# A gated cross-attention kernel on one core: FFN maximum taken chunk by chunk, second half of the queries moved into the attention loop, GpSimd's key splits moved later

## What is computed

```python
x = x + tanh(g_xattn[0]) * dtw_align(ctx, layernorm(x))      # dynamic time warping, traced back
x = x + tanh(g_ffn[0])   * bit_ffn(layernorm(x))             # below
x = x + tanh(g_xattn[1]) * attention(layernorm(x), ctx)      # 16 heads of 16, softmax over 375 keys
x = x + tanh(g_ffn[1])   * pattern_ffn(layernorm(x))         # 2048 patterns, three top-k selections
```

## Time and profile before

| what | value |
|---|---|
| median of 3 runs | 580.42 us (579.89 to 580.88) |
| the profiled execution's own time | 581.3 us |
| its span | 579.6 us |
| mean granted TensorE clock | 0.835 of full |
| busy TensorE / VectorE / ScalarE / GpSimd | 403.9 / 414.0 / 261.1 / 81.3 us |

### The profile page before, as it was taken

The page is one execution under the profiler, slowest core; times in us unless marked ns, Lnnn a source line. Parts: engine busy times, 40 slices in busy tenths (PEclk is TensorE's granted clock), DMA queues, the critical chain, the costliest instruction groups (busy, mean ns, idle before and its releaser), DMA issues.

```text
span 579.6 us, 10039 instructions
## 1 busy us (share of the span) xinstructions
PE 403.9 (70%) x3352; PEld 268.5 (46%) x3356; DVE 414.0 (71%) x1680; ACT 261.1 (45%) x674; POOL 81.3 (14%) x209
## 2 busy tenths in 40 slices
PE   2898799722249799787899999999999602503106
PEld 2557586511137455454577776676545300202003
DVE  7644999999965758997988887784354575375773
ACT  3854444712231543246465555765453352353440
POOL 6791000000024063724000000000000000000000
PEclk9998799955559799799999999999999955855556
DMA  9700003287004688410034847920860000000002
GB/s 271 230 1 1 0 2 120 94 174 158 14 2 132 105 153 159 128 50 1 2 54 69 217 68 139 185 79 2 332 247 1 1 0 2 0 1 1 1 1 63
DMA packets 33448, 47.22 MB, mean 81 GB/s; under 512 B 5477, under 2 KB 29942, under 8 KB 32246
## 3 DMA queue, kind: packets, MB, share of 16 engines
q1 hardware_dynamic: 33398, 46.58, 32.9%
HBM read 37.87 MB, written 8.60 MB: 80 GB/s over the span
## 4 chain that ended last, share of the span: by engine, by line
PE 45%; DVE 33%; ACT 12%; issue 5%; POOL 4%; DVEq 0%; POOLq 0%; ACTq 0%
PE ps L2118 8%; ACT below L1726 6%; PE ps L2082 5%; DVE PR L1028 4%; PE ps L2069 4%; PE ps L2058 4%; PE ps L1967 4%; PE ps L2044 3%; DVE R L962 2%; PE ps L1912 2%; DVE prod L1024 2%; PE ps L1828 2%; DVE PR L1026 2%; PE ps L2239 1%; DVE R L958 1%
## 5 line engine op out<-in xcount | busy, mean ns | idle before, releaser
L1242 DVE TENSOR_REDUCE negm<-ps 112x1 f32<-112x375 f32 x128 | 65.5, 543 | 9.2 <-PE ps L2058 6.0
L1700 ACT ACTIVATE E<-ps 125x448 f32<-125x448 f32 x96 | 52.0, 544 | 40.9 <-PE ps L2069 40.6
L2207 PE MATMUL ps<-cnt,same 128*128 128x7 bf16 (+3 forms) x36 | 6.2, 171 | 70.9 <-ACT below L1726 62.8
L2058 PE MATMUL ps<-ks,qs 96*112 96x375 bf16 x128 | 42.8, 345 | 1.7 <-DVE negm L1242 0.8
L1230 DVE TENSOR_REDUCE acts<-gel 128x4 f32<-128x448 f32 x32 | 19.8, 621 | 31.2 <-ACT gel L1668 31.2
L2082 PE MATMUL ps<-E,v 125*32 125x112 f32 x768 | 42.0, 270 | 0.0
L2069 PE MATMUL ps<-qs,ks 99*125 99x112 bf16 x384 | 39.4, 225 | 1.2 <-DVE qs L1263 0.7
L2069 PEld LDWEIGHTS ps<-qs,ks 99*125 99x125 bf16 x384 | 33.7, 137 | 10.2 <-issue 6.2
L2207 PEld LDWEIGHTS ps<-cnt,same 128*128 128x128 bf16 (+1 forms) x36 | 4.0, 111 | 73.6 <-issue 73.6
L1668 ACT ACTIVATE gel<-ps 128x448 f32<-128x448 f32 x32 | 17.3, 544 | 29.3 <-PE ps L2118 29.3
L768 POOL CAST kp<-kx 128x750 bf16<-128x750 f32 x8 | 6.5, 812 | 163.5 <-ACT path L1583 125.1
(11 more groups left out here) (369 smaller groups left out, 1037.7 us busy)
## 6 DMA issues: line engine op xcount, KB each, us to landing
ks<-key_parts SPq DMA_DIRECT2D x48, 187.5 KB, 6.7
piwT<-fn_process_input_weights SPq DMA_DIRECT2D x4, 2048.0 KB, 14.9
key_parts<-kp SPq DMA_DIRECT2D x48, 93.8 KB
ctx_again<-in_ctx SPq DMA_DIRECT2D x7, 512.0 KB
keys<-kx SPq DMA_DIRECT2D x16, 187.5 KB, 2.2
kx<-keys SPq DMA_DIRECT2D x8, 375.0 KB, 6.0
ctxP<-in_ctx SPq DMA_DIRECT2D x8, 256.0 KB, 6.4
patT<-in_L_ffn_input_patterns SPq DMA_DIRECT2D x1, 2048.0 KB, 13.2
```

Source lines behind the costliest of these rows:

```text
L1242: drain(dve.tensor_reduce(negm[:, n:n + 1], bank(nm)[0:S, 0:SC], AX.X, ALU.max, negate=True), nm)
L1700: drain(fn(E[:, (KCH * f + c) % 6, :], bank(nm)[0:KC, 0:4 * S], ACT.Exp), nm)
L2058: fill(mm(bank(nm)[0:S, 0:SC], qs[0:SR, u // 4 % 3, n, :], ks[0:SR, u // 4 % 3, n, :], start=True, stop=True), nm)
```

## The change

Three edits, put in together.

1. **FFN maximum.** ScalarE writes the absolute value of chunks 0 to 5 back into their slots of `ct0`. VectorE takes a running maximum of those, five maxima of two tensors, each one chunk behind the middle tap. `hmax2` is gone. TensorE's transposes of the maximum stand ahead of the fillers, of which four are left of ten.
2. **Queries.** Before the loop only the first half is transposed, multiplied, biased and split. The second half's transposes stand in round -4, its products and ScalarE's copies in rounds -3 and -2; three fillers a round are left only in round -1. Its split goes from VectorE to GpSimd, behind the keys of batch 4.
3. **Keys of batches 5 to 7.** GpSimd splits them after the far queries and the bias adds. SyncE stores the parts of batch b + 2 and loads the keys of batch b + 4 behind the stack of batch b.

```diff
+EARLY = 5
...
-            for b in range(2, B):
+            for b in range(2, EARLY):
                 store_parts(b)
-                if b + 2 < B:
-                    load_keys(b + 2)
+                load_keys(b + 2)
                 if b == 2:
                     load_stack(2)
             for b in range(3, B):
                 wait_filled(sp, ("scoreT", 4 * b - 9, KCH - 1))
                 load_stack(b)
+                if b + 2 < B:
+                    store_parts(b + 2)
+                    if b + 4 < B:
+                        load_keys(b + 4)
...
             wait_drained(pool, ("ffn_up", 0, 1))
-            for b in range(2, B):
+            for b in range(2, EARLY):
                 split_keys(b)
+            for t in range(2):
+                wait_drained(pool, ("qT", t, 1))
+                far = slice(448, 896)
+                did(pool.tensor_tensor(qx32[:, t, far], qx32[:, t, far], qp[:, t, 0, far], ALU.subtract))
+                settle()
+                did(pool.tensor_copy(qp[:, t, 1, far], qx32[:, t, far]))
+                settle()
+                pool.tensor_tensor(qp[:, t, 2, far], qx32[:, t, far], qp[:, t, 1, far], ALU.subtract
+                                   ).then_inc(q_far_split, 1)
             wait_drained(pool, "bo")
             pool.wait_ge(ln_ready, 3 * B)
             for b in range(B):
                 pool.tensor_tensor(x[:, b, :], x[:, b, :], gbo[:, :], ALU.add).then_inc(bias_added, 1)
+            for b in range(EARLY, B):
+                split_keys(b)
...
                     if e >= 3:
                         dve.wait_ge(silu_done, e - 2)
+                        settle()
...
-                if c in (5, 8):
-
-                    e = c - 5
-                    dve.wait_ge(silu_done, e + 3)
-                    three = hs[:, e:e + 3, :].rearrange("p c t -> p t c")
-                    if e == 0:
-                        ins = dve.tensor_reduce(hmax[:, :], three, AX.X, ALU.max, apply_absolute_value=True)
+                if 4 <= c < HT + 1:
+
+                    e = c - 3
+                    dve.wait_ge(size_ready, e + 1)
+                    if e == 1:
+                        ins = tt(hmax[:, :], ct0[:, 0, :], ct0[:, 1, :], ALU.max)
                     else:
-                        did(dve.tensor_reduce(hmax2[:, :], three, AX.X, ALU.max, apply_absolute_value=True))
                         settle()
-                        dve.wait_ge(hmax_part, 1)
-                        ins = tt(hmax[:, :], hmax[:, :], hmax2[:, :], ALU.max)
-                    ins.then_inc(hmax_part, 1)
+                        ins = tt(hmax[:, :], ct0[:, e % 3, :], hmax[:, :], ALU.max)
+                    if e < HT - 3:
+                        did(ins)
+                    else:
+                        ins.then_inc(hmax_ready, 1)
...
-            for half in range(2):
-                for t in range(2):
-                    wait_drained(dve, ("qT", t, half))
-                    cols = slice(448 * half, 448 * half + 448)
...
+            near = slice(0, 448)
+            for t in range(2):
+                wait_drained(dve, ("qT", t, 0))
...
                 fn(hs[:, c, :], ct0[:, c % 3, :], ACT.Silu, bias=cb[:, c:c + 1]).then_inc(silu_done, 1)
                 if c + 3 < HT:
                     spread_taps(c + 3)
+                if c < HT - 2:
+                    act.wait_ge(silu_done, c + 1)
+                    fn(ct0[:, c % 3, :], hs[:, c, :], ACT.Abs).then_inc(size_ready, 1)
...
-            query_columns(0)
-            norm_columns(1)
-            query_columns(1)
+            query_columns(0, 0)
+            query_columns(0, 1)
...
                 if f == -3:
                     load_table(ACT.Exp)
+                if f == -4:
+                    norm_columns(1)
+                if f in (-3, -2):
+                    query_columns(1, f + 3)
...
-            keep_clock(("hidT", HT - 1, 0), 10)
-            pe.wait_ge(hmax_part, 2)
+            pe.wait_ge(hmax_ready, 1)
             hidden_transposes(("hmaxT",), hmax)
+            keep_clock(("hidT", HT - 1, 0), 4)
...
+            ln_transposes(2, "lnT2", ln2, 0)
+            query_product(0, 0)
+            query_product(0, 1)
...
-                pe.wait_ge(q_split, 2 * (u // (2 * B)) + tile + 1)
+                pe.wait_ge(q_split if u < 2 * B else q_far_split, tile + 1)
...
-                if f < 0:
+                if f == -4:
+                    ln_transposes(2, "lnT2", ln2, 1)
+                if f in (-3, -2):
+                    query_product(1, f + 3)
+                if f == -1:
                     keep_clock(("pv", 0), 3)
```

More of the change, by code:

```diff
@@ L360, in build_program @@
         hmax = rf.take("hmax", [128, TOK])
-        hmax2 = rf.take("hmax2", [128, TOK])
         q2 = Region(q2_at).take("q2", [128, HT, TOK], BF16)
@@ L485, in build_program @@
          qx_ready, sx_ready, scaled, norm_ready, rows_ready, q2_act, uu_ready, rounded, bias_added, cand_ready,
-         signs_ready, dg_ready, silu_done, s2_ready, q2_ready, hmax_part,
-         neg_ready, q_split, k_split, pv_part, cnt_ready, tie_ready, sel_ready,
+         signs_ready, dg_ready, silu_done, size_ready, s2_ready, q2_ready, hmax_ready,
+         neg_ready, q_split, q_far_split, k_split, pv_part, cnt_ready, tie_ready, sel_ready,
          gel_ready, gel_used, acts_ready, pmx_ready, pmd_ready, pexp_ready, vec, scl, pol) = [sem(n) for n in (
@@ L491, in build_program @@
              "sx_ready scaled norm_ready rows_ready q2_act uu_ready rounded bias_added cand_ready signs_ready "
-             "dg_ready silu_done s2_ready q2_ready hmax_part neg_ready q_split "
+             "dg_ready silu_done size_ready s2_ready q2_ready hmax_ready neg_ready q_split q_far_split "
              "k_split pv_part cnt_ready tie_ready sel_ready gel_ready gel_used acts_ready "
@@ L1211, in _ @@
                 normalise(b, x, ln2[:, b, :])
-            for half in range(2):
-                for t in range(2):
-                    wait_drained(dve, ("qT", t, half))
-                    cols = slice(448 * half, 448 * half + 448)
[L1217 to L1221, removed]
+            near = slice(0, 448)
+            for t in range(2):
+                wait_drained(dve, ("qT", t, 0))
+                did(tt(qx32[:, t, near], qx32[:, t, near], qp[:, t, 0, near], ALU.subtract))
+                settle()
+                did(dve.tensor_copy(qp[:, t, 1, near], qx32[:, t, near]))
+                settle()
+                tt(qp[:, t, 2, near], qx32[:, t, near], qp[:, t, 1, near], ALU.subtract).then_inc(q_split, 1)
             a0 = quarters(acts[0][:, :])
@@ L1642, in norm_columns, with query_columns @@
                     drain(fn(ln2T[:, h, 448 * half:448 * half + 448], bank(nm)[:, 0:448], ACT.Copy), nm)
[L1644 to L1652, removed]
+            def query_columns(half, t):
+                nm = ("qT", t, half)
+                wait_filled(act, nm)
+                cols = slice(448 * half, 448 * half + 448)
+                did(fn(qx32[:, t, cols], bank(nm)[:, 0:448], ACT.Identity, bias=bqs[:, t:t + 1], scale=HD ** -0.5))
+                drain(fn(qp[:, t, 0, cols], bank(nm)[:, 0:448], ACT.Identity, bias=bqs[:, t:t + 1],
+                         scale=HD ** -0.5), nm)
             half_root(2, 0)
@@ L2023, in _, with query_product @@
                 keep_clock(("lnT2", 0, 0), 3)
-            for half in range(2):
-                ln_transposes(2, "lnT2", ln2, half)
+            def query_product(half, t):
+                nm = ("qT", t, half)
+                claim(pe, nm)
                 for h in range(DH):
                     wait_drained(pe, ("lnT2", h, half))
[L2028 to L2034, removed]
+                    ins = mm(bank(nm)[:, 0:448], wqT[:, h, 128 * t:128 * t + 128],
+                             ln2T[:, h, 448 * half:448 * half + 448], start=(h == 0), stop=(h == DH - 1))
+                fill(ins, nm)
+            ln_transposes(2, "lnT2", ln2, 0)
+            query_product(0, 0)
+            query_product(0, 1)
             def queries(u):
```

## The result

The changed kernel took 579.34 us (median of 20 runs, 573.44 to 583.24) against 581.35 for the kernel before (20 runs, 579.89 to 583.65): a ratio of 0.9949, 95% interval 0.9928 to 0.9970. The ratio leaves out the changed kernel's three longest runs, counted as a slower state since they lie over 1.5% above its fastest; the medians of all twenty differ by 2.0 us. So it is faster by a third to a half of a per cent, a third to a half of the 6 us that were forecast, and its runs spread more widely than those before. The profiled execution took 580.88 around a span of 579.2. What the runs at 573 to 576 lost, no profile shows.

A forecast was written before the change was run, and what follows sets the result against it. TensorE was taken to bound convolution and early attention, VectorE leading between until the quantised hidden is out. Terms -6.2 - 3.0 + 3.2 = -6.0 took 581.3 to 575.3, 0.9 lower for the median: 574.4 us, range 571.0 to 578.8.

The forecast's parts named there:

- FFN maximum: End of the FFN convolution: last middle taps start at 230.05 instead of 232.76, a gain of 2.7 us.
- Keys out of the tail: FFN tail: without GpSimd's key splits, gains of 2.3, 0.8 and 0.4 us, making 6.2 with the FFN maximum.
- The 0.8 in it for the clock: Fillers between the hidden's halves: the granted clock no longer falls to 0.50, worth 0.8 us with the fillers' rounding.
- Queries: Start of attention: second half's query work moved between rounds, a gain of 3.0 us, bounds 2.0 and 4.5.
- 10 and 7 to 9 as signs: Start of attention: first score product 10 us earlier in absolute time, first maxima split 7 to 9 earlier.
- GpSimd beside attention: Maxima splits in attention: GpSimd holds VectorE, costing 1.4, 1.5 and 0.3 us, sum 3.2; second split held 2.4.
- rival 1: Maxima splits: holding nearly free, as steps slip between or strided casts aren't held; 571.2 to 571.7 us, chance 0.27.
- The sum up to 304 us: Whole change: -6.2 for the tail, -3.0 for queries, +3.2 for holding, together -6.0 us.
- I cost the queue at nothing: SP's queue in attention: six stores take 3.74 us to issue, stack loads keep their place, so no cost.
- The sign I had named for being wrong: Attention: a stack load that TensorE waits for, one of several signs against the forecast.
- the 9.2 that the forecast had ahead of its subtraction: FFN tail and start of attention: gains of 6.2 and 3.0 us before the 3.2 for holding.
- rival 2: Splits at three batches: VectorE waits out full turns, 9.5 against 9.2 us; 580.7, no change, chance 0.08.

The follow-up runs named there:

- e6_queries_only: The kernel before with the second edit (queries) alone: 581.43 us, ratio 1.0001.
- e1_pat_late: The changed kernel with the 2 MB load of the patterns moved two batches later, behind the seventh stack: 574.47 us, ratio 0.9895.
- e12_before_pat_late: The kernel before with the patterns loaded two batches later, nothing else: 580.96 us, ratio 1.0004.
- e11_ffn_pat_late: The kernel before with the running FFN maximum alone and the patterns loaded two batches later: 580.18 us, ratio 0.9996.
- e7_fillers: The changed kernel with patterns late, plus 7 fillers before the first query stack and 8 before the first maxima product: 575.88 us, ratio 0.9916.
- e4_ffn_only: The kernel before with the first edit (running FFN maximum) alone: 583.25 us, ratio 1.0047.
- e2_store7_late: The changed kernel with batch 7's six stores moved from behind the stack of batch 5 to behind that of batch 6: 579.98 us, ratio 0.9973.

## Why the prediction was right and wrong

**FFN maximum: right.** The convolution stays full (29.91 of 30, ScalarE 18.2), no table is loaded between Silu and absolute value, and from the first middle tap to the last 24.9 us go instead of 27.6: 2.65, forecast 2.7.

**Keys out of the tail: right.** The held steps fell to 0.17, the clock stayed at 1.00. From first tap to the update of x the gain of the first two terms together is 49.84 - 43.56 = 6.3, forecast 6.2. The 0.8 in it for the clock is not shown: e6_queries_only had the full clock in that stretch with the keys still in it, and was no shorter (50.2).

**Queries: right, a little undersized.** From the update of x to the first maxima split it is 24.5 instead of 28.3: 3.8, forecast 3.0. Each of my rounds was slightly too long. The first score product came 11.7 earlier and the first split 11.0, 0.9 of each not the change's, where I had given 10 and 7 to 9 as signs.

**GpSimd beside attention: right in kind, the clock left out.** The first split is held 1.3 (forecast 1.4), the second 1.5 (2.4), the third not at all. The strided casts are held as well, 1.43 for the longest, which goes against my rival 1. The Trainium skill (GPSIMD Engine Reference, Key points) names instructions in a 2-port perf mode or with two SBUF inputs; this cast has one input, so the trace agrees only if it ran in such a mode, which no row shows. But the wait is followed by the 1.2 GHz level (0.64 from 278 to 282) in an attention that TensorE bounds. Between the two splits 2.5 us are lost in the changed kernel and 3.3 in e1_pat_late; 3.2 was my whole sum for the holding, without the clock.

**The sum up to 304 us** was -6.0; measured -7.15 in the profiles, -6.2 from a common start.

**What failed is one sentence**: "I cost the queue at nothing; a late stack would show as a TensorE wait." I reasoned that each stack kept its place and that stored parts had four rounds, and set the 3.74 us of six stores against the keys of batch 7 alone. I did not look at what stands behind the stores of batch 6: the 2 MB of patterns, and then stack 5. The 13 us between these two were the cover, just as long as the load. The stores took 3.7 us of it and the load grew from 13.2 to 21.0, so the last load of the stack landed at 340.2, with TensorE out of work from 334.85. I had counted the time on SyncE's queue, not the bytes behind it. That term was 5.5 us of waiting and the rest of the 7.1 at half clock. It is a cost of the third edit itself; that the stage came 7 us earlier moved stack and patterns alike. The sign I had named for being wrong, a stack load that TensorE waits for, is the one that showed.

With the patterns later (e1_pat_late) the same kernel is at 574.47, where the forecast was 574.4. That match is in part luck: in its profile the lead at the first batch's normalisation is 4.2 when both are counted from the first middle tap, not 6.0, since the clock fell at two places and took back more than the queries gave beyond their term; the first middle tap itself came 1.6 earlier, which is not the change's. With the holding gone too it is 1.6%, some 9.2 us, under the kernel before, against the 9.2 that the forecast had ahead of its subtraction, though in the profiles those two terms measure 6.3 and 3.8, together 10.1.

What I underrated is a small gain or none, for which rival 2 had 0.08. None of the three edits wins alone, and two of them lose: each gain in the tail lands in a stretch whose clock, turn-taking or DMA gives it back.

## What to carry to other kernels

When an edit puts transfers on a queue, list what stands behind them there: a large load that was just through when the next urgent one came has no cover to give away, and a few microseconds of small stores ahead of it become the next wait. A large load that nobody needs soon belongs behind the small ones that are; here moving it was worth 4.9 us. Work moved to an idle engine should be given its own waits, so that it stays clear of the few short steps that everybody waits for; here two waits on GpSimd were worth 3 us. And one edit timed by itself can lose where the three together win, so read where each one's gain went before dropping it.

## What was not expected of the hardware

The same TensorE instructions in the same order kept the clock at 1.00 from 282 to 290 in the kernel before and in e12_before_pat_late, and fell to 0.72 and 0.50 in e11_ffn_pat_late, where they come 3 us earlier. I can't say from these runs what decides; in e7_fillers, fillers in two of the waits did not prevent such a fall. e1_pat_late had a fall to 0.57 from 262 to 266 that the changed kernel, with the same instructions there, did not have.

TensorE can wait for nothing that the profile names: 1.89 us at 325 in e4_ffn_only, with the DMA engines at a share of 0.99, and 1.37 at 304 in e2_store7_late, at 0.49. The last transfer on the instruction queue stands up to 1.5 us ahead of either wait, and none within it. In e11_ffn_pat_late, with the patterns later, 0.22 of the first are left. In the kernel before, 0.75 us of this kind stood at 360 with the DMA engines at 0.02, so a loaded DMA makes such a wait longer at most, and is not needed for one.
